# Router logits: 32x32 block transposes by VectorE and four small DMAs in place of TensorE transposes

## What is computed

```python
x = x + attn(layernorm(x))
xt = layernorm(x)
logits = xt @ router_w                      # 256 -> 8 experts
probs  = softmax(logits)
top    = top_k(probs, 2); top = top / sum(top)
out    = (gelu(xt @ w1 + b1) @ w2 + b2) * sum(combine(top))   # one scale per token
x = x + out
```

## Time and profile before

| | before |
|---|---|
| median of 3 runs | 1197.71 us (1197.66 to 1198.62) |
| the profiled execution | 1198.14 us, its span 1196.3 us |
| PE busy | 1183.7 us, 99% of the span |
| DVE busy | 961.9 us, 80% |
| ACT busy | 884.3 us, 74% |
| POOL busy | 640.1 us, 54% |
| granted PE clock | 1.0 in every slice |

### The profile page before, as it was taken

The page is one execution under the profiler, slowest core; times in us unless marked ns, Lnnn a source line. Parts: engine busy times, 40 slices in busy tenths (PEclk is TensorE's granted clock), DMA queues, the critical chain, the costliest instruction groups (busy, mean ns, idle before and its releaser), DMA issues. The chain is left out here.

```text
span 1196.3 us, 29198 instructions
## 1 busy us (share of the span) xinstructions
PE 1183.7 (99%) x11347; PEld 1040.4 (87%) x11347; DVE 961.9 (80%) x1714; ACT 884.3 (74%) x1914; POOL 640.1 (54%) x809
## 2 busy tenths in 40 slices
PE   8999999999999999999999999999999999999999
PEld 6778888888888888888888888888888888988988
DVE  7788789878988888888888888889888987666644
ACT  6888788888887888788888887888888884334432
POOL 5776556555655565556555655555555674222221
PEclk9999999999999999999999999999999999999999
DMA  4222111311121113111311131113111232121100
GB/s 132 66 77 66 34 40 30 95 25 35 36 88 35 37 37 89 37 37 37 89 37 36 37 89 37 36 37 89 37 37 37 72 86 79 36 69 39 36 19 36
DMA packets 35240, 62.91 MB, mean 53 GB/s; under 512 B 5920, under 2 KB 12576, under 8 KB 35104
## 3 DMA queue, kind: packets, MB, share of 16 engines
q1 hardware_dynamic: 35104, 61.05, 19.0%
HBM read 19.08 MB, written 8.39 MB: 23 GB/s over the span
## 5 line engine op out<-in xcount | busy, mean ns | idle before, releaser
L927 POOL TENSOR_SCALAR prob<-prob,rowinv 128x512 f32<-128x512 f32 x512 | 350.2, 699 | 290.6 <-DVE rowinv L1116 290.2
L836 ACT ACTIVATE prob<-ps,negmax 128x512 f32<-128x512 f32 x512 | 347.0, 686 | 34.1 <-DVE negmax L1111 29.7
L1035 DVE TENSOR_TENSOR pT_lo<-ps,pT_hi 128x512 fp32r<-128x512 f32 (+1 forms) x384 | 320.4, 862 | 26.0 <-ACT pT_hi L829 21.3
L1111 DVE TENSOR_REDUCE negmax<-ps 128x2 f32<-128x1024 f32 x256 | 311.1, 1215 | 1.3 <-PE ps L524 1.2
L826 ACT ACTIVATE pT_hi<-ps 128x1024 fp32r<-128x1024 f32 x128 | 131.7, 1029 | 99.3 <-issue 98.7
L552 PEld LDWEIGHTS ps<-identity,prob 64*128 64x128 f32 x4096 | 154.7, 138 | 57.9 <-issue 18.2
L552 PE MATMUL ps<-identity,prob 64*128 64x64 f32 x4096 | 177.1, 226 | 3.4 <-DVE vbuf L1035 2.6
L518 PE MATMUL ps<-nat 64*128 64x512 f32 x1024 | 172.1, 413 | 1.5 <-ACT prob L836 0.5
L566 PE MATMUL ps<-pT_hi,vbuf 128*128 128x256 f32 x1024 | 164.8, 283 | 1.7 <-DVE pT_lo L1035 1.6
L566 PE MATMUL ps<-pT_lo,vbuf 128*128 128x256 f32 x1024 | 164.5, 283 | 0.0
L829 ACT ACTIVATE pT_hi<-ps 128x512 fp32r<-128x512 f32 x256 | 140.4, 610 | 16.5 <-PE ps L552 16.5
(11 more groups left out here) (119 smaller groups left out, 2307.1 us busy)
## 6 DMA issues: line engine op xcount, KB each, us to landing
att_hi_v<-halves_out SPq DMA_DIRECT2D x128, 128.0 KB, 2.3
att_lo_v<-halves_out SPq DMA_DIRECT2D x128, 128.0 KB, 2.3
xres<-in_x SPq DMA_DIRECT2D x8, 512.0 KB, 3.4
x_scratch<-xres SPq DMA_DIRECT2D x8, 512.0 KB, 3.1
out_y<-f_o SPq DMA_DIRECT2D x15, 256.0 KB, 2.0
xin<-in_x SPq DMA_DIRECT2D x7, 512.0 KB, 3.8
wstage<-in_w SPq DMA_DIRECT2D x4, 512.0 KB, 3.6
wstage<-in_w_qkv SPq DMA_DIRECT2D x6, 256.0 KB, 3.1
```

The costliest lines, as they stand in the source:

```text
L836: act.activation(prob[:, n % NPROB, j * SEQ:(j + 1) * SEQ], ps[:, PS_SCORE[n % 2] + j, :], ACT.Exp, bias=negmax[:, n % 4, j:j + 1], accum_ ...
L927: return pool.tensor_scalar(dst, src, scalar, 1.0, ALU.mult, ALU.mult)
L1035: return dve.tensor_tensor(dst, full, hi, ALU.subtract)
L1111: dve.tensor_reduce(negmax[:, n % 4, :], ps[:, PS_SCORE[n % 2]:PS_SCORE[n % 2] + 2, :], AX.X, ALU.max, negate=True).then_inc(s_max, 1)
```

## The change

PE's transposes of the logits and ACT's copy ahead of them are gone. DVE turns the logits' rows 0 to 31 of bank 4 in 32x32 blocks into an SBUF tile `r_blocks` of 32 partitions (`turn_logits`). SP then issues four DMAs (`spread_logits`), one for each group of 32 partitions, each 32 partitions by 4 pieces of 64 bytes (8 KB), into `r_parts`. `routing_shift` waits for all four, and has three operations in place of four, since it adds the two halves straight from SBUF. On DVE, `turn_logits(c+1)` and `routing_shift(c+1)` now stand behind `finish(c, 0)`; for sequence 0, `turn_logits(0)` takes the place of `routing_shift(0)`, which moves behind the four `last_out` blocks. On SP, `spread_logits(c+1)` stands between the two stores of c. PE's waits on `s_frs` (logits shifted) become waits on `s_flt` (logits turned).

```diff
+            def spread_logits(c):
+                sp.wait_ge(s_flt, c + 1)
+                if c >= 1:
+                    sp.wait_ge(s_frs, c)
+                blocks = r_blocks[:, :, 0:2 * EXPERTS].rearrange("p (t g) e -> p g t e", t=TT)
+                for g in range(P // QUAD):
+                    sp.dma_start(r_parts[g * QUAD:(g + 1) * QUAD], blocks[:, g]).then_inc(s_frt, 16)
...
             sp.dma_start(b2_sb[:, :], b2_rows).then_inc(s_b2, 16)
+            spread_logits(0)
...
                 store_out(c, 0)
+                if c + 1 < B:
+                    spread_logits(c + 1)
                 store_out(c, 1)
...
                 if c >= 1:
-                    pe.wait_ge(s_frs, c)
+                    pe.wait_ge(s_flt, c)
...
-            def transpose_logits(c):
-                pe.wait_ge(s_flt, c + 1)
-                for t in range(TT):
-                    ins = pe.transpose(ps[:, PS_ROUTER, t * 2 * EXPERTS:(t + 1) * 2 * EXPERTS],
-                                       r_logitT[:, t * P:(t + 1) * P], identity[0:2 * EXPERTS, 0:2 * EXPERTS])
-                ins.then_inc(s_frt, 1)
...
                 down(c, 2)
-                if c + 1 < B:
-                    transpose_logits(c + 1)
                 down(c, 3)
...
-            def copy_logits(c):
-                act.wait_ge(s_frm, c + 1)
-                act.activation(r_logitT[:, :], ps[0:2 * EXPERTS, PS_ROUTER, :], ACT.Copy).then_inc(s_flt, 1)
...
+            def turn_logits(c):
+                dve.wait_ge(s_frm, c + 1)
+                if c >= 1:
+                    dve.wait_ge(s_frt, 16 * (P // QUAD) * c)
+                dve.transpose(r_blocks[:, :, :].rearrange("p j e -> p (j e)"), ps[0:QUAD, PS_ROUTER, :])\
+                    .then_inc(s_flt, 1)
+
             def routing_shift(c):
-                dve.wait_ge(s_frt, c + 1)
-                logits = ps[:, PS_ROUTER, 0:TT * 2 * EXPERTS].rearrange("p (t e) -> p t e", t=TT)
-                link(dve.tensor_copy(r_half[:, :, :], logits[:, :, EXPERTS:]))
-                link(dve.tensor_tensor(r_logit[:, :, :], logits[:, :, 0:EXPERTS], r_half[:, :, :], ALU.add))
+                dve.wait_ge(s_frt, 16 * (P // QUAD) * (c + 1))
+                link(dve.tensor_tensor(r_logit[:, :, :], r_parts[:, :, 0:EXPERTS], r_parts[:, :, EXPERTS:], ALU.add))
...
                     if c == 0 and f == TT - 1:
                         ffn_normalise(1)
-                        routing_shift(0)
+                        turn_logits(0)
...
                         aux_done(*block_of_out)
+                    routing_shift(0)
                     routing_weight(0)
...
-                if c + 1 < B:
-                    routing_shift(c + 1)
                 finish(c, 0)
                 if c + 1 < B:
+                    turn_logits(c + 1)
+                    routing_shift(c + 1)
                     routing_weight(c + 1)
                 finish(c, 1)
```

## The result

The changed kernel took 1202.61 us (median of 7, 1201.08 to 1203.81) against 1197.71 before: a ratio of 1.0036, 95% interval 1.0026 to 1.0047. It is slower by 4.9 us, where I forecast 1.3 less and a range up to 1201.0. Its profiled execution is its fastest run, 1201.08 us with a span of 1199.3; that alone is 2.9 above the profiled execution of before.

A forecast was written before the change was run, and what follows sets the result against it. PE, busy 99% of the span, was taken to bound the kernel; 4.26 us removed from its queue, less a 3.0 us first-period wait and none later, gave 1.29 us less: median 1196.4, range 1194.9 to 1201.0.

The forecast's parts named there:

- What it removes: On PE's queue: 0.53 us in each of seven periods and 0.55 for sequence 0, 4.26 us in all.
- Block transpose: On DVE: turning the logits takes 0.68 us, bounds 0.44 and 1.37, the latter for two passes.
- The chain o = L - T: From block transpose end (T) to first addition behind the four DMAs (L): 3.62 us, bounds 3.26 and 4.25.
- the margin of 0.18: In later periods PE waits only if the chain exceeds 3.80 us; at 3.62 about 0.2 us is left.
- The first period: At c = 0, normalising comes later within the period, so PE waits 3.0 us for the chain at up(1, 2).
- so the last attention blocks, the store, the reload and the normalising move 0.5 earlier: First period: DVE does less from 1003.65, so normalising ends at 1019.1 instead of 1019.58.
- The later periods: Periods c = 1 to 6: PE doesn't wait, with 0.2 us left.
- L + 7.0: Later periods: end of the gelu needed at up(c+1, 5), 7.0 us after the first addition behind the DMAs starts.
- six later periods: Periods c = 1 to 6, each charged any chain time beyond 3.80 us in the gain formula.
- The clock: Rival: a 3 us stop drops PE to 1.2 GHz for a while, up to 10.9 us more; chance 0.03.
- a wait in each period: Rival: late DVE and table load stop PE at up(c+1, 2); loss passes 2.4 us from chain 4.30; chance 0.17.
- The price of each 0.1 us: Once the chain exceeds 3.80 us, each further 0.1 us costs 0.7 us.

The follow-up runs named there:

- d_no_dma: Changed kernel without the four small DMAs per sequence and the wait for them, the addition reading zeros; 1194.77 us against 1198.67 before the change.
- c_base_later: Changed kernel with base(c+1) on DVE moved behind hidden_lo(c+1, 2); 1202.07 us against 1198.67 before the change.
- g_twice: Changed kernel with each of the four small DMAs issued twice, first to a spare tile; 1223.66 us against 1198.80 before the change.
- e_early_turn: Changed kernel with logits turned before normalising, route(c+1) earlier and the spread issued ahead of the store; 1195.30 us against 1198.80 before the change.

## Why the prediction was wrong, step by step

**What it removes: right.** 4.26 us by starts of matmuls; d_no_dma showed 3.9, and 0.3 of the rest is a wait for the last attention block.

**Block transpose: right.** 0.69 for 0.68, and one operation, not two passes.

**The chain o = L - T: 3.79 for 3.62.** The last issue followed the first 1.93 later (1020.92 to 1022.85), since the first took 0.60 like the others, for 1.79 from the earlier trace rows; the landing and the start of the addition behind it took 1.83 for 1.8. Within the bounds, and enough to use up the margin of 0.18 that I had found in the later periods.

**The first period: right in kind, 3.16 for 3.0.** But two of its terms were off, in opposite directions, and that the wait came so close is partly luck. I let normalising move 0.5 earlier, because VectorE does less at 1003.65; it moved 0.1, from 1018.20 to 1018.12:

```profile
1018.12 1.39 DVE L1027 TENSOR_SCALAR xn<-xres,ln_mv,ln_scale 128x256 f32<-128x256 f32 x4 [1.14 <-POOL ln_scale L920]
```

The step that failed is "so the last attention blocks, the store, the reload and the normalising move 0.5 earlier". Ahead of them stand the last `hidden_lo`, which wait for POOL's high parts. Before, three of these took 0.62 each (1.87 together); now the third took 1.83 and the other three 0.61 to 0.66:

```profile
1003.00 3.65 POOL L932 TENSOR_SCALAR pT_hi<-prob 128x512 fp32r<-128x512 f32 x4
...
1004.25 1.83 POOL L932 TENSOR_SCALAR pT_hi<-prob 128x512 fp32r<-128x512 f32 x1
1004.35 1.24 DVE L1031 TENSOR_TENSOR pT_lo<-prob,pT_hi 128x512 fp32r<-128x512 f32 x2
```

The second row of POOL is the third of the four in the first. It is longer by the 1.2 us in which VectorE's two `hidden_lo`, started earlier than before, ran beside it; the next `hidden_lo` waited for it until 1006.11, and the last attention blocks began at 1007.72, for 1007.75 before. The other term went the other way: PE arrived 0.3 later at its first up of sequence 1 (1021.72 for 1021.4), which shortened its wait but not the time.

**The later periods: wrong, and this is the main step.** I wrote "with L = T + 3.62 there is 0.2 us left and PE doesn't wait". PE lost 0.53 in each, all that the change had brought it. Three things, less the margin of 0.18, add up to it: 0.17 more chain; 0.41 in `hidden_lo(c+1, 0)`, 1.10 for 0.69, which no part of the sum had; and 0.11 for a restart of PE, which I had at nothing, since a matmul that had to wait is followed by its next one after 0.34 and not 0.23. (The restart at up(2, 2) costs 0.11 too, but makes the wait at up(2, 5) shorter by as much.) So the step that failed is the sum of the path to the gelu that up(c+1, 5) needs: L + 7.0 in the forecast, L + 7.42 in the profile (1049.12 to 1056.54).

I had taken the duration of `hidden_lo(c+1, 0)`, 0.68, from the row at 1050.49, in which DVE was ahead: POOL's `hidden_hi` started at 1050.90 beside it, and took 0.74 for its usual 0.62. In the changed kernel it starts 0.1 us behind the start of a `hidden_hi` on POOL, since DVE is late and POOL isn't. In c_base_later, where it starts earlier, it takes 0.69. Which of the two is held up isn't settled by which record starts first: at 1004.25 POOL's started 0.1 ahead, too, and was the one that became longer. The Trainium skill ("SBUF — State Buffer", Who interferes with whom) says that a VectorE instruction with two SBUF inputs contends with a GpSimd instruction that reads SBUF; `hidden_lo` and `hidden_hi` are such a pair, and these durations agree. So a late engine isn't only late: it meets work that it had been ahead of.

I also counted six later periods; there are five, since c = 6 has no normalising ahead of its logits and its chain starts 1 us earlier.

**The late landing: not foreseen.** One period has a chain about 1 us longer, 0.6 us more time in the profile of the changed kernel.

**The clock: foreseen as a rival with 0.03, and true in part.** Half the clock lasted 3 us, not a whole up block, and cost 1.3 at the median.

The sum: -3.9 for what leaves PE, +3.2 first wait, five later periods at 0.5 to 0.6 together +2.7, late landing +0.6, clock +1.3, is +3.9, where three measurements gave 4.3 to 4.9. In the first profile, whose clock stayed at 1.0, the starts of PE's ups leave nothing over: the first period has 3.37 more than without the transposes (24.22), the five later ones together 3.44, the late landing in them, and all of PE's work ends 2.9 later than before, as the spans do (3.0). That is 0.3 more than the terms above; the rest of the medians, 0.1 to 0.7, is open. Of the rivals, "a wait in each period" was the one that came, but the wait that counts is at up(c+1, 5) and not at up(c+1, 2), and it came not by a longer transpose or landing, but by a collision that no part of the sum had.

The price of each 0.1 us was about right: I said 0.7 for each 0.1 beyond the margin, 18 for the 2.57 of g_twice, which gave 20 with two falls of the clock and a later `route(1)` in it. What was wrong was to forecast from the safe side of an edge that lay 0.2 us away with a slope of 7.

## What to carry to other kernels

Moving a small transpose from TensorE to a block transpose and DMAs frees little time on TensorE and puts a chain of about 3.8 us (four issues of 0.64, a landing of 1.8) on the path; it pays only if the chain starts that much before its result is needed, as e_early_turn shows. Look first for the period in which the input is latest, and at what a late engine will run beside; a margin smaller than one such collision is none. Where a wait must stay, a wait of 2 to 3 us can also cost TensorE's clock.

## What the hardware showed that I had not expected

- TensorE's granted clock fell from 2.4 to 1.2 GHz at waits of 3.1 us and even 2.1 us, in some executions and not in others of the same kernel, stayed low for about 3 us, and never fell in ten runs in which the wait was filled with matmuls.
- Four DMAs of 8 KB in 64-byte pieces within SBUF took 0.60 us each to issue, as much as those of 128 KB in the earlier trace rows, and 1.8 to land, only 0.5 less than the median of those.
- A `hidden_lo` of 0.69 us took 1.10 beside a POOL instruction, and POOL's of 0.62 took 1.83 beside two `hidden_lo`: one of the two engines lost about the time for which the other went on.
- A landing of 1.8 us became 2.7 where the trace has one packet on the queue of instructions in the same stretch.
